# Lead-in of a two-layer kernel: low gate weights and w1's rounding on GpSimd, i·z of chunk 0 on VectorE, one table for the first tanh and exp

## The reference

```python
x = x + attn(layernorm(x), W, b, input_bias, scale)
x = x + ffn(layernorm(x), gamma, beta, fc1_q, fc1_scales, fc1_bias, fc2_q, fc2_scales, fc2_bias)

# attn: x is already normalised
pre = x @ W + b                                  # 256 -> 4 * 256
i_pre, f_pre, o_pre, z = split(pre, 4)
i = 10 * tanh((i_pre + input_bias) / 10);  f = -softplus(f_pre);  o = sigmoid(o_pre);  tz = tanh(z)
# over the steps:
m_next = max(f + m, i);  i_s = exp(i - m_next);  f_s = exp(f + m - m_next)
c = f_s * c + i_s * tz;  n = f_s * n + i_s;  h = o * c / (n + 1e-6)
# then h / rms(h) * scale

# ffn: a layernorm of its own, gamma and beta
w1 = (fc1_q - 128) * fc1_scales                  # 256 -> 1024
y = silu(h @ w1 + fc1_bias)
w2 = (fc2_q - 128) * fc2_scales                  # 1024 -> 256
return residual + 0.5 * (y @ w2 + fc2_bias)
```

## Time and profile before

| | us |
|---|---|
| median of 3 runs | 321.24 (321.14 to 321.33) |
| profiled execution, its own time | 321.89 |
| its span, first to last instruction | 320.0 |
| PE busy in the span | 303.9 (95%) |
| PEld busy | 263.8 (82%) |
| DVE busy | 267.4 (84%) |
| ACT busy | 229.7 (72%) |
| POOL busy | 118.1 (37%) |

### The profile page before, as it was taken

How to read it: one execution, slowest core, us unless ns; L and a number is a source line. 1 busy time by engine, 2 the same in 40 slices (tenths; PEclk the granted TensorE clock), 3 DMA queues, 4 the chain that set the end, 5 groups by cost and what they waited for, 6 DMA issues and landing times.

```text
span 320.0 us, 4813 instructions
## 1 busy us (share of the span) xinstructions
PE 303.9 (95%) x1760; PEld 263.8 (82%) x1760; DVE 267.4 (84%) x474; ACT 229.7 (72%) x372; POOL 118.1 (37%) x126
## 2 busy tenths in 40 slices
PE   0999999999899997999999999999999999999996
PEld 0787788887898877988899888988899899899896
DVE  3998999999999999998969987888959899863531
ACT  3598966999599938489694978779593876941930
POOL 2162035002483179015920187014991156154000
PEclk9999998999999999799999999999999999999999
DMA  7990000000000020020000200010000100100101
GB/s 274 357 374 14 1 0 2 0 0 0 2 1 2 33 98 3 34 98 2 1 2 33 98 0 2 33 36 0 1 2 25 43 0 0 68 0 5 63 0 68
DMA packets 10951, 14.21 MB, mean 44 GB/s; under 512 B 688, under 2 KB 10160, under 8 KB 10672
## 3 DMA queue, kind: packets, MB, share of 16 engines
q1 hardware_dynamic: 10512, 13.12, 11.8%
q10 hardware_dynamic: 416, 0.79, 0.7%
HBM read 9.71 MB, written 4.19 MB: 43 GB/s over the span
## 4 chain that ended last, share of the span: by engine, by line
PE 45%; DVE 20%; issue 14%; POOL 12%; ACT 6%; DMA 3%; POOLq 0%; DVEq 0%; SPq 0%
PE mm_ps L221 7%; PE mm_ps L219 7%; PE mm_ps L220 7%; PE z_ps L220 6%; PE z_ps L219 6%; PE z_ps L221 6%; POOL rows L1034 3%; DVE rec L672 2%; DVE g L729 2%; DMA rows<-x 2%; POOL rec L1001 2%; DVE rows L737 2%; POOL g L1019 2%; DVE bn L742 2%; DVE rec L687 2%
## 5 line engine op out<-in xcount | busy, mean ns | idle before, releaser
L219 PE MATMUL z_ps<-w_hi,y_hi 128*128 128x256 f32 x248 | 71.3, 288 | 1.4 <-issue 1.4
L220 PE MATMUL z_ps<-w_lo,y_hi 128*128 128x256 f32 x248 | 70.4, 284 | 0.0
L221 PE MATMUL z_ps<-w_hi,y_lo 128*128 128x256 f32 x248 | 70.4, 284 | 0.0
L765 DVE TENSOR_TENSOR y_lo<-y,y_hi 128x512 fp32r<-128x512 f32 x64 | 43.2, 687 | 12.2 <-ACT y_hi L504 11.7
L501 ACT ACTIVATE y<-mm_ps,b_all 128x512 f32<-128x512 f32 x60 | 41.3, 688 | 13.4 <-PE mm_ps L288 9.8
L219 PEld LDWEIGHTS z_ps<-w_hi,y_hi 128*128 128x128 f32 x248 | 47.5, 191 | 1.9 <-issue 1.8
L220 PEld LDWEIGHTS z_ps<-w_lo,y_hi 128*128 128x128 f32 x248 | 47.2, 190 | 0.1
L221 PEld LDWEIGHTS z_ps<-w_hi,y_lo 128*128 128x128 f32 x248 | 47.1, 190 | 0.0
L1005 POOL TENSOR_TENSOR rrms<-meansq,minus_half 128x4 f32<-128x4 f32 x8 | 9.0, 1122 | 96.5 <-DVE meansq L723 96.5
L219 PE MATMUL mm_ps<-gt_hi,w_hi 128*128 128x512 f32 x108 | 43.2, 400 | 0.0
L220 PE MATMUL mm_ps<-gt_lo,w_hi 128*128 128x512 f32 x108 | 42.8, 396 | 0.0
(11 more groups left out here) (154 smaller groups left out, 669.4 us busy)
## 6 DMA issues: line engine op xcount, KB each, us to landing
out<-rows SPq DMA_DIRECT2D x15, 256.0 KB, 2.1
rows<-x SPq DMA_DIRECT2D x7, 512.0 KB, 6.4
q<-fc_q SPq DMA_DIRECT2D x2, 1024.0 KB, 12.1
s<-fc_scales SPq DMA_DIRECT2D x1, 1024.0 KB, 11.2
wg_raw<-fc_scales SPq DMA_DIRECT2D x1, 1024.0 KB, 11.1
wg_raw<-w_gates SPq DMA_DIRECT2D x1, 512.0 KB, 5.5
wg_raw<-w_gates ACTq DMA_DIRECT2D x1, 512.0 KB, 5.8
rows<-x ACTq DMA_DIRECT2D x1, 256.0 KB, 3.4
```

The lines of the kernel that those rows point to most:

```text
L219: pe.matmul(dst, wh[w_at], ah[a_at], start=start, stop=False)
L220: pe.matmul(dst, wh[w_at], al[a_at], start=False, stop=False)
L221: return pe.matmul(dst, wl[w_at], ah[a_at], start=False, stop=stop)
L765: dve.tensor_tensor(y_lo[:, j], y[:, j % YBUFS], y_hi[:, j].bitcast(F32), ALU.subtract).then_inc(y_lo_done, 1)
```

## The change

- POOL makes both blocks of `wg_lo`, between the roots of chunks 0 and 1. The first two tiles of gates get a function of their own, `first_two_gates`: all high·high matmuls of both tiles, then those with x's low part, then those with `wg_lo`.
- DVE makes `gate_bias` before x_low(0) in another form: two operations on one column with a scalar from `col`, one multiplication by a constant, two copies. The sums of chunk 1's statistics also stand before x_low(0), the means behind it.
- i·z of chunk 0 is made on DVE, between the maximum of chunk 0 and x_low(1).
- w1 is rounded as a whole on POOL (128x2048), no longer half on DVE and half on ACT.
- ACT loads the table `exp_and_others`, which serves tanh and exp, and then sigmoid's: two loads instead of three.
- x of chunk 1 is turned after tile 5 of chunk 0, x of chunk 2 after tile 4 of chunk 1, h of chunk 0 after tile 0 of chunk 2. ACT's order follows: x_normalised(2) before the o tiles of chunk 0, x_high(2) before the table load, square_sums(0) after tile 0 of chunk 2.

```diff
--- before.py
+++ after.py
@@ -248,13 +248,31 @@
                         continue
                     for k in range(KD):
                         pe.wait_ge(xt_hi_done, at(c, 2, k + 1))
-                        if c == 0:
-                            pe.wait_ge(wg_split_lo, k + 1)
                         pe.matmul(dst, wg_hi[:, k, f], x_hi[:, k], start=(k == 0), stop=False)
                         pe.matmul(dst, wg_lo[:, k, f], x_hi[:, k], start=False, stop=False)
                     for k in range(KD):
                         pe.wait_ge(xt_lo_done, at(c, 2, k + 1))
                         ins = pe.matmul(dst, wg_hi[:, k, f], x_lo[:, k], start=False, stop=(k == KD - 1))
+                    ins.then_inc(pre_done, 1)
+
+            def first_two_gates():
+
+                x_hi, x_lo = xt(0)
+                f = [slice(GATE_ORDER[j] * P, GATE_ORDER[j] * P + P) for j in range(2)]
+                for k in range(KD):
+                    pe.wait_ge(wg_split_hi, k + 1)
+                    pe.wait_ge(xt_hi_done, k + 1)
+                    for j in range(2):
+                        pe.matmul(gate_bank(0, j), wg_hi[:, k, f[j]], x_hi[:, k], start=(k == 0), stop=False)
+                for k in range(KD):
+                    pe.wait_ge(xt_lo_done, k + 1)
+                    for j in range(2):
+                        pe.matmul(gate_bank(0, j), wg_hi[:, k, f[j]], x_lo[:, k], start=False, stop=False)
+                pe.wait_ge(wg_split_lo, KD)
+                for j in range(2):
+                    for k in range(KD):
+                        ins = pe.matmul(gate_bank(0, j), wg_lo[:, k, f[j]], x_hi[:, k], start=False,
+                                        stop=(k == KD - 1))
                     ins.then_inc(pre_done, 1)
 
             def fc1(c, tiles):
@@ -370,15 +388,16 @@
                     if n == TT - 1:
                         ins.then_inc(xt_ready, 1)
 
-            gates(0, range(0, 5))
+            first_two_gates()
+            gates(0, range(2, 6))
             x_turned(1)
-            gates(0, range(5, GJ))
-            gates(1, range(0, 7))
+            gates(0, range(6, GJ))
+            gates(1, range(0, 5))
             x_turned(2)
-            gates(1, range(7, GJ))
-            gates(2, range(0, 2))
+            gates(1, range(5, GJ))
+            gates(2, range(0, 1))
             h_turned(0)
-            gates(2, range(2, GJ))
+            gates(2, range(1, GJ))
             shifted_bias()
             g_turned(0)
             fc1(0, range(0, 6))
@@ -505,37 +524,33 @@
 
             act.dma_start(rows[:, 0, 2:TT], x_view[0, 0, :, 2:TT]).then_inc(x_landed[0], 16)
             act.dma_start(wg_raw[:, 1], w_gates[P:2 * P, :]).then_inc(wg_in[1], 16)
-            act.preload_act_table_set("sigmoid_and_others")
+            act.preload_act_table_set("exp_and_others")
             for k in range(KD):
                 act.wait_ge(wg_in[k], 16)
                 act.activation(wg_hi[:, k], wg_raw[:, k], ACT.Copy).then_inc(wg_split_hi, 1)
             x_high(0)
-            act.wait_ge(bias_ready, 3)
+            act.wait_ge(bias_ready, 5)
+
 
             gates(0, I_TILES)
-            act.preload_act_table_set("natural_log_exp_and_others")
             exp_i(0)
             act.preload_act_table_set("sigmoid_and_others")
-            gates(0, F_TILES)
+            gates(0, range(2, 6))
             x_high(1)
-            gates(0, range(4, 7))
-            act.wait_ge(w1_scaled, 1)
-            act.activation(w1_hi[:, 1], w1_f[:, 1], ACT.Copy).then_inc(w1_rounded, 1)
-            gates(0, range(7, GJ))
             x_normalised(2)
+            gates(0, range(6, GJ))
 
             gates(1, I_TILES)
             act.preload_act_table_set("natural_log_exp_and_others")
             reciprocal(0)
             exp_i(1)
+            x_high(2)
             act.preload_act_table_set("sigmoid_and_others")
-            gates(1, F_TILES)
-            x_high(2)
-            gates(1, range(4, GJ))
-
-            gates(2, I_TILES)
+            gates(1, range(2, GJ))
+
+            gates(2, range(0, 1))
             square_sums(0)
-            gates(2, range(2, GJ))
+            gates(2, range(1, GJ))
             g_normalised(0)
             g_high(0)
             act.preload_act_table_set("natural_log_exp_and_others")
@@ -792,30 +807,25 @@
             dve.memset(carry[:, :, 1:3], 0.0).then_inc(carry_zeroed, 1)
             ln1(0)
             x_normalised(0)
-            for k in range(KD):
-                dve.wait_ge(wg_split_hi, k + 1)
-                dve.tensor_tensor(wg_lo[:, k], wg_raw[:, k], wg_hi[:, k].bitcast(F32), ALU.subtract
-                                  ).then_inc(wg_split_lo, 1)
+            dve.wait_ge(col_in, 16)
+            for j in range(2):
+                dve.tensor_scalar(gate_bias[:, j:j + 1], col[:, j:j + 1], col[:, COL_IB + j:COL_IB + j + 1], 1.0 / CAP,
+                                  ALU.add, ALU.mult).then_inc(bias_ready, 1)
+            dve.tensor_scalar(gate_bias[:, 2:4], col[:, 2:4], -1.0, None, ALU.mult).then_inc(bias_ready, 1)
+            dve.tensor_copy(gate_bias[:, 4:6], col[:, 6:8]).then_inc(bias_ready, 1)
+            dve.tensor_copy(gate_bias[:, 6:8], col[:, 4:6]).then_inc(bias_ready, 1)
+
+            ln1_sums(1)
             x_low(0)
-            dve.wait_ge(col_in, 16)
-            dve.scalar_tensor_tensor(out=gate_bias[:, 0:2], in0=col[:, 0:2], scalar=1.0,
-                                     in1=col[:, COL_IB:COL_IB + KD], op0=ALU.mult, op1=ALU.add).then_inc(bias_ready, 1)
-            dve.tensor_scalar(gate_bias[:, 2:4], col[:, 2:4], -1.0, None, ALU.mult)
-            dve.tensor_copy(gate_bias[:, 4:6], col[:, 6:8])
-            dve.tensor_copy(gate_bias[:, 6:8], col[:, 4:6]).then_inc(bias_ready, 1)
-            dve.wait_ge(bias_ready, 2)
-            dve.tensor_scalar(gate_bias[:, 0:2], gate_bias[:, 0:2], 1.0 / CAP, None, ALU.mult).then_inc(bias_ready, 1)
-
-            ln1(1)
+            ln1_means(1)
             ln1(2)
             x_normalised(1)
             dve.wait_ge(q1_in, 16)
             dve.wait_ge(s1_in, 16)
             dve.scalar_tensor_tensor(out=w1_f, in0=q1[:], scalar=-ZERO_POINT, in1=s1[:],
                                      op0=ALU.add, op1=ALU.mult).then_inc(w1_scaled, 1)
-            dve.wait_ge(w1_scaled, 1)
-            dve.tensor_copy(w1_hi[:, 0], w1_f[:, 0]).then_inc(w1_rounded, 1)
             maximum(0, range(KD))
+            input_times_z(0)
             x_low(1)
             denominators(0, range(KD))
             divisor(0)
@@ -826,7 +836,7 @@
             x_low(2)
             h(0)
 
-            dve.wait_ge(w1_rounded, KD)
+            dve.wait_ge(w1_rounded, 1)
             dve.tensor_tensor(w1_lo[:], w1_f, w1_hi[:].bitcast(F32), ALU.subtract).then_inc(w1_ready, 1)
             maximum(1, range(0, 1))
             mean_square(0)
@@ -1040,9 +1050,14 @@
                                pattern=[[-1, P]], channel_multiplier=1).then_inc(ident_ready, 1)
             pool.wait_ge(half_ready, 1)
             ln1_root(0)
+            for k in range(KD):
+                pool.wait_ge(wg_split_hi, k + 1)
+                pool.tensor_tensor(wg_lo[:, k], wg_raw[:, k], wg_hi[:, k].bitcast(F32), ALU.subtract
+                                   ).then_inc(wg_split_lo, 1)
             ln1_root(1)
             ln1_root(2)
-            input_times_z(0)
+            pool.wait_ge(w1_scaled, 1)
+            pool.tensor_copy(w1_hi[:], w1_f).then_inc(w1_rounded, 1)
             pool.wait_ge(b2_in, 16)
             pool.tensor_scalar(b2_bc[:], b2_bc[:], 0.5, 0.0, ALU.mult, ALU.add).then_inc(b2_halved, 1)
             rms_root(0)
```

## The result

The changed kernel takes **325.34 us** (median of 4 runs, 324.64 to 326.23) against 321.19 of the kernel before in the same session (4 runs, 321.05 to 321.33): ratio 1.0106, 95% interval 1.0082 to 1.0131. It is 4.1 us slower. The forecast was 321.1 with a range to 323.3. What came is rival 4, to which the prediction gave 0.04. The profiled execution took 324.76, with a span of 322.9.

What follows compares the result with a forecast made beforehand. The later of chain (C, 52.56) and PE (P, 52.01) was taken to set the turning of g; PE at 52.4 gives -0.15 us, 321.1 on the median. Own range 320.7 to 321.7; 8 in 10, 320.0 to 323.3.

Steps and rivals of the forecast that it cites:

- rival 4: At the start, POOL's wg_lo also holds off DVE's xn, the last two ending 3.8 us late: 325.1, chance 0.04.
- What bounds the kernel, and the carry to the end: A shift at the turning of g of chunk 0 (52.56) should arrive at the end about one for one.
- C: Time when the chain through DVE, POOL and ACT has g of chunk 0 ready: 52.56, forecast 52.2 to 52.4.
- P: Time when PE is through chunk 2's gates and shifted_bias, free to turn g: 52.01, forecast 52.4.
- The start: Stretch from DVE's xn (ending 8.85) to PE's tile 2, forecast at 14.46 instead of 14.12: PE +0.34.
- rival 1: At the start, DVE's last bias copy is caught between POOL's halves and waits 2.4 us more: 323.3, chance 0.17.
- the forecast's own case: At the start, bias multiply and both copies wait until 10.2, then slip in between POOL's halves; price 1.3 us, chance 0.45.
- The table and the cast: Before chunk 0's scans, ACT drops a table load of 1.28; POOL's w1 cast takes 1.7, 1.6 of it blocking DVE.
- PE's wait for y_lo at chunk 1 (0.7): Near 25, PE was to wait 0.7 us at chunk 1's first tiles, making PE +1.0 in all.
- Rival 2: Near the scans, POOL's w1 cast runs beside xt_lo without blocking DVE, 1.2 to 1.6 earlier: 320.3, chance 0.23.
- Rival 3: Behind PE's wait of 2.0 near 127, the clock stays at 2.4 GHz, saving 1.7 us: 319.4, chance 0.08.
- The first at the cold clock: At the start, only the first of PE's first four matmuls, from 10.44, was taken to run at the cold clock.

Runs made afterwards that it cites:

- e4: Changed kernel, with DVE's xn of chunks 0 and 1 taking constants 1.0 and 0.0 instead of scalars read from SBUF; 325.99 us (1 run).
- e10: Changed kernel, with POOL's wg_lo held until chunk 0's xn is done, bias operations behind x_low(0), and w1 rounded wholly by ACT; 321.48 us, ratio 0.9999.
- e2: Changed kernel with one wait more: POOL starts wg_lo only when all four xn of chunk 0 are done; 325.27 us, ratio 1.0105.
- e1: Changed kernel with wg_lo back on DVE ahead of x_low(0), and the bias and chunk 1's sums behind it; 323.25 us, ratio 1.0060.
- e7: Changed kernel with POOL's wg_lo held until chunk 0's xn is done, and the bias operations moved behind x_low(0); 322.41 us, ratio 1.0018.
- e6: Kernel before, with only the one table for tanh and exp from the change; 322.26 us, ratio 1.0012.
- e8: Kernel before, with the one table for tanh and exp and w1 rounded by ACT alone; 322.62 us, ratio 1.0021.
- e5: Changed kernel with wg_lo back on DVE and w1 rounded as before, half on DVE, half on ACT; 322.42 us, ratio 1.0015.

## Why the prediction was wrong

- **What bounds the kernel, and the carry to the end: right.** The turning of g moved 3.9, x of chunk 5 then 4.3, and the span followed, less the 1.4 that came back at 132 to 138. The later of C and P sets it, as put: ACT ends g at 55.46, while PE is busy until 56.6, so it is P.
- **"DVE ends xn at 8.85", and everything in "The start" that stands on it: wrong, and this is the step that failed.** The bound "xn is not held off" rested on its rate: one element a cycle, hence no second port, hence no wait. What the runs show in its place: in the changed kernel two of the four xn took 2.44 and 2.43 for 0.41, each until a half of POOL was over, and xn ended at 13.16. e4 shows that the speed was no ground for the bound: xn waits for POOL at 0.28 as at 0.41 each. The reading of the rate was weak by itself. It set four instructions of 256 with eight scalars from SBUF against one cast of 1024 with none, and counted their starts as rate; by the estimate under e4 xn runs as fast an element as the cast, so the trace did not contradict the rule of the Trainium skill that the prediction named. The Trainium skill had it right (SBUF — State Buffer, Who interferes with whom): it counts tensor_scalar, copy and cast between SBUF tiles as holders of the pair of ports that DVE shares with GpSimd, whoever comes first keeping it for its whole instruction. This case agrees in every row of tensor_scalar and copy that met POOL: 2.44, 2.43 (xn), 2.30, 2.33 (two columns), 1.18 and 1.11 beside a fill. It also says that an operation with at most one input in SBUF, outside the modes with two ports, does not contend; xt_lo, with its other input in PSUM, is such a one and keeps its 1.29 in e10. That operations on one column stay out as well is e10's own row (0.33 for two). I had let the trace overrule a rule when the trace had no xn beside a POOL operation in it, only its speed.
- **Price and place of rival 4: right** (xn 3.8 late, 325.1; measured 4.3 and 325.34). It had the third and fourth xn held off; it was the second and third. That 325.1 lies so near is in part luck: the medians differ by 4.1, but the two profiled executions only by 2.9. Its chance of 0.04 was the error. The sum for it had been worked out; an honest weight, with a rule for it and only an inference from the rate against it, would have stretched the range to it.
- **POOL's halves of 2.41, the bias held off, rival 1:** the halves took 2.52 and 2.38; the bias met them only once xn was out of the way (e2), and then as rival 1 had it, a copy caught for 2.33. So the forecast's own case, one held operation and both copies slipping in, did not occur in the one trial it had.
- **The table and the cast:** the table saves its 1.28 (only one load, 21.09, between exp and f). The cast took 1.90 where 1.7 was taken, and its block of 1.6 is in e1 (4.04 - 2.46). In the changed kernel itself it cost only 0.3: f came at 23.6, when the cast had 0.5 left to run, and the two scans took 2.73 for 2.46.
- **PE's wait for y_lo at chunk 1 (0.7):** absent after (DVE and PE were late together), 1.07 in e1.
- **Rival 2 (the cast hides)** did not come: in e1 and e7 it met a scan, and in the changed kernel it had most of its time to itself only because f was late. **Rival 3 (the clock)** came in part: behind the wait of 2.2 the clock stayed at 2.4 GHz, with 1.4 back there where the rival had 1.7, as a discount on the loss. But its lower stretch near the turning of g grew from 3.5 to 6.5. That the four runs lie near 324.7 (two) and near 326.1 (two) would fit an execution that gets it and one that does not; only one was profiled, so this is not shown, and the mean clock does not sort them (0.989 at 324.76 and at 325.92).
- **"The first at the cold clock":** by its pace, right, although the profile shows a granted clock of 1.00 from 8.03 on: 0.63 a matmul is what rows with a granted clock of 0.50 show. But it held for four matmuls and not for the first alone, and how long it holds differs between executions, which the sum took as fixed.

## What to carry to other kernels

Before an operation goes to GpSimd, list what VectorE does in the same microseconds: an xn, a copy or a constant multiplication between SBUF tiles, of 256 elements or of 2, waits for the whole GpSimd instruction, so a short and urgent operation costs as much as the long one it meets. Do not take the speed of an operation as a sign that it runs free; look for a row of it beside GpSimd. Put beside it what was seen to run free (statistics, an input in PSUM), and hold GpSimd back by one semaphore rather than let it start early. A saving ahead of such a pair moves the moment at which they meet, so look at the meeting again after every shift, also where the edit itself touches neither engine.

## What was not expected of the hardware

- A multiplication and a copy of 128x2 took 2.30 and 2.33 us beside GpSimd, 0.15 alone; two operations on 128x1 took 0.33 for both, while GpSimd's second half ran (e10, 11.96).
- A fill, which reads nothing, holds tensor_scalar off as a subtraction does (1.18 and 1.11 for 0.41).
- Between two GpSimd instructions back to back VectorE gets the held operation through and at most one short one behind it (a copy in e2, nothing more between the two long xn); a scan behind another lets GpSimd in just so (e1, e6).
- tensor_scalar of 128x256 in fp32 takes 0.28 us with constants (e4) and 0.41 with two scalars from SBUF; one scalar costs about 0.05 us an instruction even on one column (0.12 from start to start, 0.07 with constants on two).
- The first matmuls run at 0.63 us for 0.39, and from nearly the same start (10.44, 10.46, 10.46) for another 1.5, 3.6 or 5.9 us (kernel before, e8, e5), with the granted clock shown as 1.00 in all three. Matmuls under a granted clock of 0.50 take 0.63 too (58.94 to 61.50 in the changed kernel), so the record of the clock seems not to hold at the start.
- Rounding 128x2048 took 1.90 us on GpSimd unhindered, and 1.91 on ScalarE (e10, 25.28).
